# Output projection of head pairs as seven block products instead of eight, in a latent-attention transformer layer

## What is computed

```python
x = x + attn(layernorm(x))          # x: (8, 512, 512)
x = x + ffn(layernorm(x))           # 1536 wide
# attn, for each batch and each of 16 heads:
scores = (q_nope @ k_nope.T + q_pe @ k_pe.T) / sqrt(192)
attn   = softmax(scores, axis=-1)
out    = concat_over_heads(attn @ v)          # 512 tokens x (16 * 128)
return out @ wo.T                             # 512 x 512
```

## Time and profile before

| what | value |
|---|---|
| median of 3 runs | 2230.14 us (2228.98 to 2230.31) |
| span of the profiled execution | 2228.8 us, 1.3 us under the median |
| granted TensorE clock, mean | 0.999 |
| PE busy, matmuls | 2205.4 us, 99%, 10977 |
| DVE, ACT, POOL busy | 70%, 48%, 45% |
| DMA, mean | 98 GB/s |

### The profile page before, as it was taken

One profiled execution on the slowest core, in us unless ns is written; L12 is line 12 of the kernel. 1 busy time (PEld: TensorE's weight loads), 2 busy tenths in 40 slices (PEclk: granted clock), 3 DMA queues, 4 the chain that ended last, 5 costly groups with the idle time before them and its releaser, 6 DMA issues.

```text
span 2228.8 us, 34908 instructions
## 1 busy us (share of the span) xinstructions
PE 2205.4 (99%) x10977; PEld 1026.8 (46%) x10977; DVE 1557.8 (70%) x3227; ACT 1066.6 (48%) x2345; POOL 1001.5 (45%) x688
## 2 busy tenths in 40 slices
PE   7999999999999999999999999999999999999999
PEld 5444544445444454444544445444454445444454
DVE  7888887776477764777648775587755877467773
ACT  6667564554255542555325553355443554345532
POOL 4657465453355524454244642536334363343322
PEclk9999999999999999999999999999999999999999
DMA  7868336562175631756216561365614564145530
GB/s 248 188 124 150 88 71 142 106 124 51 23 151 105 122 53 34 145 105 127 44 43 146 106 121 29 73 123 106 118 25 104 106 115 95 24 104 109 106 65 19
DMA packets 703800, 219.42 MB, mean 98 GB/s; under 512 B 685520, under 2 KB 685776, under 8 KB 702672
## 3 DMA queue, kind: packets, MB, share of 16 engines
q1 hardware_dynamic: 703696, 218.09, 47.7%
HBM read 40.78 MB, written 8.39 MB: 22 GB/s over the span
## 4 chain that ended last, share of the span: by engine, by line
PE 93%; DVE 3%; ACT 1%; DMA 1%; POOL 1%; issue 1%; SPq 0%; DVEq 0%; POOLq 0%
PE bank L853 13%; PE bank L291 11%; PE bank L293 11%; PE bank L292 11%; PE scores L863 7%; PE scores L663 5%; PE scores L293 5%; PE scores L291 5%; PE scores L292 5%; PE bank L674 4%; PE bank L675 4%; PE bank L676 4%; PE scores L660 3%; PE bank L840 1%; PE bank L689 1%; PE scores L557 1%
## 5 line engine op out<-in xcount | busy, mean ns | idle before, releaser
L1716 POOL TENSOR_TENSOR arena<-arena 128x1024 f16<-128x1024 f32 x256 | 545.7, 2132 | 620.3 <-ACT arena L1079 620.3
L1077 ACT ACTIVATE arena<-scores,shift 128x512 f32<-128x512 f32 x512 | 357.5, 698 | 535.0 <-DVE shift L1429 494.8
L1449 DVE SCALAR_TENSOR_TENSOR arena<-bank,rden,arena 128x512 f32<-128x512 f32 x508 | 347.9, 743 | 137.0 <-PE bank L293 137.0
L1427 DVE TENSOR_REDUCE mx<-scores 128x1 f32<-128x512 f32 x512 | 352.5, 689 | 20.5 <-PE scores L293 16.7
L1079 ACT ACTIVATE arena<-scores,shift 128x512 f16<-128x512 f32 x512 | 358.6, 700 | 0.0
L853 PE MATMUL bank<-arena,WFF 128*128 128x512 f16 x1392 | 313.5, 379 | 0.8 <-DVE arena L1601 0.6
L1774 POOL TENSOR_TENSOR arena<-arena 128x512 f16<-128x512 f32 x96 | 114.4, 1191 | 255.6 <-ACT arena L1152 255.6
L853 PEld LDWEIGHTS bank<-arena,WFF 128*128 128x128 f16 x1392 | 135.9, 98 | 164.1 <-DVE arena L1601 2.3
L291 PE MATMUL bank<-WVO,arena 128*128 (+1 forms) x512 | 194.2, 379 | 2.4 <-DVE arena L1222 1.2
L1222 DVE SCALAR_TENSOR_TENSOR arena<-bank,arena 128x512 f16<-128x512 f32 (+1 forms) x263 | 176.2, 670 | 29.1 <-ACT arena L1070 24.4
L663 PE MATMUL scores<-arena 128*128 128x512 f16 x512 | 195.4, 382 | 0.0
(11 more groups left out here) (159 smaller groups left out, 3480.5 us busy)
## 6 DMA issues: line engine op xcount, KB each, us to landing
arena<-arena SPq DMA_TRANSPOSE x712, 3.2
arena<-w_ffn SPq DMA_DIRECT2D x24, 384.0 KB, 3.5
arena<-x SPq DMA_DIRECT2D x8, 1024.0 KB, 5.6
out<-arena SPq DMA_DIRECT2D x32, 256.0 KB, 2.0
arena<-x SPq DMA_DIRECT2D x14, 512.0 KB, 4.4
WVO<-w_o SPq DMA_DIRECT2D x4, 1024.0 KB, 8.2
arena<-w_nope SPq DMA_DIRECT2D x4, 768.0 KB, 9.1
arena<-down_scale SPq DMA_DIRECT2D x8, 256.0 KB, 3.3
```

What stands on the lines that cost most here:

```text
L1077: act.activation(P32[:, t, :], SC[:, t, :], ACT.Exp, scale=EXP_SCALE, bias=shift[:, t:t + 1], accum_out=esum[:, par, t:t + 1]).then_inc(s[ ...
L1427: dve.tensor_reduce(mx[:, t:t + 1], SC[:, t, :], AX_X, ALU.max).then_inc(s["mxr"], 1)
L1449: dve.scalar_tensor_tensor(out=XR[:, t, :], in0=banks[t][:, :], scalar=by[:, t:t + 1], in1=XR[:, t, :], op0=ALU.mult, op1=ALU.add).then_in ...
L1716: pool.tensor_tensor(PL[:, par, two, :], P32[:, two, :], PH[:, par, two, :], ALU.subtract).then_inc(s["pl"], 1)
```

## The change

Heads are taken in pairs (even head e, odd head o), for the first 14 heads of batches 2 to 7; the last two heads of each of these batches, and all of batches 0 and 1, keep the old projection. With the tokens in two halves and the output columns in two halves of 256, a pair's contribution is a 2 x 2 by 2 x 2 block product. It is now formed by seven block products instead of eight, each with 2 x 3 matmuls of 256 columns, from sums and differences of the context blocks (X32, XP) and of the weight blocks.

- **Weights.** In batch 1 POOL forms the four sums of weight blocks of each pair (`block_sums`, ten operations of 256 elements; `block_sums_lo`, one of 1024), ACT their high halves (`sum_hi`), and SP writes seven blocks per pair to DRAM (`w_duo`). From batch 2 on WVO's memory is reused, and SP loads each pair's blocks (the four early ones 512 KB together, the three late ones 384 KB) ahead of use.
- **Softmax sums.** Because heads are now mixed in the products, the reciprocals are applied to the context, where tokens are columns. DVE makes them (`row_of_sums`, three small operations), ACT spreads them (`row_twice`, 1024 elements), SP turns them by a transposing DMA, POOL adds the two halves (`row_sum`), DVE multiplies the context by the row (`context_by_row`).
- **Sums of contexts.** POOL forms them once a pair (`context_sums`, four operations of 256 and a cast of 1024; `context_sums_lo`, one of 1024); ACT and DVE make high and low halves of the plain blocks (`context_hi`, `context_lo`).
- **Order.** In each head PE's values product now comes last, and the products of a pair come one head later than its second context: four early ones in even heads, three late ones in odd heads. DVE adds eight quadrants per pair (`add_block`), four in each head.
- The next input's scaling moves from POOL to DVE and ACT. The head loops of PE and ACT are unrolled from batch 2 on.

```diff
+            def duo_product(j, x, w, k, start):
+                for t in range(2):
+                    dst = DBANK[k][:, t * HB:(t + 1) * HB]
+                    for m, (p, q) in enumerate(((0, 0), (0, 1), (1, 0))):
+                        r = pe.matmul(dst, lhsT=XP[j % 2][:, p, x, tile(t)], rhs=WB[:, q, w, :],
+                                      start=(start and t == 0 and m == 0), stop=(m == 2), skip_group_check=True)
+                return r
+EARLY = [(X_E1, W_B11, 0, True), (X_S1, W_T1, 1, True), (X_O1, W_B21, 2, True), (X_S2, W_T2, 0, False)]
+LATE = [(X_S3, W_T3, 0, False), (X_S4, W_B22, 1, False), (X_O2, W_T4, 2, True)]
+        DBANK = (BO, BT, BC)
+            def duo_early(b, j):
+                n, base = (b - B_PLAIN) * N_DUO + j + 1, b * (NH * NT) + 8 * j
+                pe.wait_ge(s["w_early"], 16 * n)
+                pe.wait_ge(s["ctl"], b * N_CT + 2 * j + 2)
+                pe.wait_ge(s["outr"], base)
+                for k, (x, w, bk, start) in enumerate(EARLY):
+                    if x == X_S1:
+                        pe.wait_ge(s["x_lo"], n)
+                    if x == X_O1:
+                        pe.wait_ge(s["cth"], b * N_CT + min(2 * j + 3, 2 * N_DUO))
+                    if x == X_S2:
+                        pe.wait_ge(s["outr"], base + 1)
+                    duo_product(j, x, w, bk, start).then_inc(s["outp"], 1)
+            # PE
+            def duo_step(b, i):
+                scores(b, i // 2, i % 2)
+                if i >= 4 and i % 2 == 0:
+                    duo_early(b, (i - 4) // 2)
+                elif i >= 5:
+                    duo_late(b, (i - 5) // 2)
+                absorb(i + 2, b * NH + i + 2)
+                values(b, *before(i // 2, i % 2))
+            # in values()
+                if b >= B_PLAIN and dst is BC:
+                    h = pair * 2 + par
+                    pe.wait_ge(s["cth"], n)
+                    pe.wait_ge(s["outr"], b * (NH * NT) + (0 if h < 3 else 8 * ((h - 3) // 2) + (3 if h % 2 else 8)))
+            # DVE
+            def context_by_row(b, i):
+                n, j, par = b * N_CT + i, i // 2, i % 2
+                dve.wait_ge(s["ctp"], n + 1)
+                dve.wait_ge(s["row"], (b - B_PLAIN) * (2 * N_DUO) + i + 1)
+                k = (b - B_PLAIN) * N_DUO + j
+                if par == 0 and k > 0:
+                    dve.wait_ge(s["x_lo"], k)
+                x = X32[:, X_O1:X_O2 + 1] if par else X32[:, X_E1:X_S3 + 1:X_S3 - X_E1]
+                dve.scalar_tensor_tensor(out=x, in0=BC[:, :].rearrange("p (m n) -> p m n", m=2), scalar=1.0 / ROW_SCALE,
+                                         in1=ROW[:, par].rearrange("p (m n) -> p m n", m=2), op0=ALU.mult,
+                                         op1=ALU.mult).then_inc(s["cth"], 1)
+            def duo_step(b, i, part=None):
+                g = b * NH + i
+                if i >= 2:
+                    context_by_row(b, i - 2)
+                    context_lo(b, i - 2)
+                maxima(g)
+                if part in (0, 1, 2):
+                    next_norm(b, part)
+                if i >= 4 and i % 2 == 0:
+                    adds_early(b, (i - 4) // 2)
+                elif i >= 5:
+                    adds_late(b, (i - 5) // 2)
+                row_of_sums(b, i)
+                qa_lo(g + 2, i % 2)
+                if part in (2, 3):
+                    next_norm(b, part + 1)
+            # ACT
+            def duo_step(b, i):
+                context_hi(b, i - 2)
+                probs(b * NH + i, i % 2, False)
+                qa_hi(b * NH + i + 2, i % 2)
+                row_twice(b, i)
+            # POOL, for each head i
+                        if i >= 3 and i % 2:
+                            context_sums(b, (i - 3) // 2)
+                        head(base + i, i % 2, (0,))
+                        if 1 <= i <= 2 * N_DUO:
+                            row_sum(b, i - 1)
+                        head(base + i, i % 2, (1,))
+                        if i >= 3 and i % 2:
+                            context_sums_lo(b, (i - 3) // 2)
+            # POOL, batch 1
+                    if plain and not first and i >= 2:
+                        if i % 2 == 0:
+                            block_sums(i // 2 - 1)
+                        else:
+                            block_sums_lo(i // 2 - 1)
+            # SP, after the transposes of head i
+                    if not plain:
+                        if i < 2 * N_DUO:
+                            row_of_head(b, i)
+                        if i == 0:
+                            early_blocks(b, 0)
+                            late_blocks(b, 0)
+                        elif i >= 4 and i % 2 == 0:
+                            early_blocks(b, i // 2 - 1)
+                        elif i >= 5:
+                            late_blocks(b, i // 2 - 1)
             # PE, last heads of batches 2 to 6
+                if b >= B_PLAIN:
+                    duo_early(b, N_DUO - 2)
                 latent("q", 0)
+                if b >= B_PLAIN:
+                    values(b, final - 1, 1)
                 scores(b, final, 1)
+                    duo_late(b, N_DUO - 2)
                 values(b, final, 0, BQ)
+                if b >= B_PLAIN:
+                    duo_early(b, N_DUO - 1)
+                    duo_late(b, N_DUO - 1)
```

More of the change, by code:

```diff
@@ L259, in build @@
             "gu", "th", "gt", "ft", "fh", "fl", "dn", "yt", "yo", "yv",
+            "t_plain", "t_sum", "t_hi", "t_lo", "t_out", "rdc", "dup", "row_t", "row", "x_hi", "x_sum", "x_lo", "w_early", "w_late",
         )}
@@ L464, in batch @@
                         weight_chunk(chunk_of(i) + 2)
+                if plain and not first:
+                    sums_of_blocks(N_DUO - 1)
                 sp.wait_ge(s["ctp"], (b + 1) * N_CT)
@@ L1098, in attention @@
                 rot_hi(b, N_ROT_FFN)
+                if not plain:
+                    row_twice(b, 0)
                 if first:
@@ L1107, in attention @@
                 qa_hi(base + 3, 1)
+                if not plain:
+                    row_twice(b, 1)
                 if first:
@@ L1709, in keys_rotated_lo, with head @@
                                    ALU.subtract).then_inc(s["kpl"], 1)
-            def head(g, par):
-                for half in range(2):
+            def head(g, par, halves=range(2)):
+                for half in halves:
                     two = slice(2 * half, 2 * half + 2)
@@ new lines, in context_sums, with step @@
+            def context_sums(b, j):
+                k, n = (b - B_PLAIN) * (5 * N_DUO) + 5 * j, b * N_CT + 2 * j
+                def step(to, x, y, op, after):
+                    if after:
+                        pool.wait_ge(s["x_sum"], k + after)
+                    pool.tensor_tensor(to, x, y, op).then_inc(s["x_sum"], 1)
+                pool.wait_ge(s["cth"], n + 2)
+                pool.wait_ge(s["outp"], b * (NH * NT) + 8 * j - 8)
+                x = [X32[:, m] for m in range(N_BLK)]
+                step(x[X_S1], x[X_S3], x[X_O2], ALU.add, 0)
+                step(x[X_S3], x[X_E1], x[X_S3], ALU.subtract, 1)
+                step(x[X_S2], x[X_S1], x[X_E1], ALU.subtract, 0)
+                step(x[X_S4], x[X_O1], x[X_S2], ALU.subtract, 3)
+                pool.wait_ge(s["x_sum"], k + 4)
+                pool.sem_inc(s["turn"])
+                pool.tensor_copy(XP[j % 2][:, 0, X_S3:], X32[:, X_S3:]).then_inc(s["x_sum"], 1)
@@ L1746, in attention, with context_sums_lo @@
+            def context_sums_lo(b, j):
+                pool.wait_ge(s["x_sum"], (b - B_PLAIN) * (5 * N_DUO) + 5 * j + 5)
+                pool.tensor_tensor(XP[j % 2][:, 1, X_S3:], X32[:, X_S3:], XP[j % 2][:, 0, X_S3:],
+                                   ALU.subtract).then_inc(s["x_lo"], 1)
+            def attention(b, last, first, plain):
                 base = b * NH
```

305 lines of the change are left out of this document (267 added, 38 removed).

## The result

The changed kernel takes **2445.0 us** (median of four runs, 2441.1 to 2445.7) against 2230.2 of the kernel before beside it: ratio 1.0955, 95% interval 1.0940 to 1.0971. The profiled execution spans 2443.6 us, 214.8 more than before.

What follows compares the result with a forecast made beforehand. It took PE, busy 99%, as the bound. Gain and waits came to 130.5 us over batches 2 to 6, 23.8 in batch 7, 14 in batch 1: +168 on 2228.8 gave 2398 us, range 2262 to 2470.

Steps and rivals of the forecast that it cites:

- The gain: PE in batches 2 to 7: 42 matmuls of 256 columns replace 24 of 512, saving 0.59 us per pair, 24.6 in all.
- The even heads' wait for x_lo: Even heads: context_by_row waits for GpSimd's low halves, delaying maxima and first add; PE waits about 2.0 us.
- Head 4: Same wait in head 4, with norm statistics between maxima and adds and short heads 1 to 3 before: 5.2 us.
- Head 6: Even-head wait in head 6 of batches 2 to 6: 1.4 us.
- The next rows' scaling on VectorE: Next rows' norm moved from POOL, at most 0.67 us on DVE at head ends, where it waits for PE: costs nothing.
- The odd heads' 0.55: Odd heads: the values product waits for all eight adds, done at 8.4 us against PE's 7.9; PE waits 0.55 us.
- head 5's 1.1: Odd-head wait in head 5, made longer by the norm's aggregates: 1.1 us.
- Start: Start of batches 2 to 7: queued loads delay probability rows; 5.5 us at values(1) and 2.4 at values(2).
- Tail: Head 15: early products of pair 6 wait 3.2 us for x_lo, late ones 1.0 us for adds or the w_late load.
- Batch 1: POOL overloaded by block sums beside next_norm in heads 8 and 10, delaying ACT: 14 us, between 5 and 20.
- More than this: Rival, chance 0.05: DMA late in every head or a lower granted clock in gaps; both together might cost 80 more, 2480.
- Contended low halves: Rival, chance 0.15: odd heads' context_lo waits for a POOL operation, 0.4 us more before the maxima, +12, 2410.

Runs made afterwards that it cites:

- e1: Changed kernel with GpSimd's low halves of the context sums (context_sums_lo) moved from the odd head's end to right behind context_sums: 2419.2 us.
- e7: Changed kernel with the even head's second half written to a block of its own, so VectorE no longer waits for GpSimd's low halves: 2361.4 us.
- e11: e1 with VectorE's third norm part moved from head 5 to 6, and its row tiles from heads 6 to 9 to heads 6 and 8: 2399.4 us.
- e15: e7 with head 15's late blocks before its transposes, first blocks behind head 2's, low halves early in head 15, third norm part after head 6: 2305.3 us.
- e3: Changed kernel with the first pair's weight blocks loaded after head 2's transposes instead of after head 0's: 2422.1 us.
- e12: e13 with e3's later first blocks, the residual load moved from behind head 0's transposes to head 3's, and norm statistics behind the adds: 2383.5 us.
- e13: e7 with e1's early low halves, and head 15's late weight blocks issued before its transposes: 2361.7 us.
- e8: Changed kernel with extra matmuls that nobody reads put into PE's idle places, 82 in each of six batches: 2413.9 us.
- e18: e15 with GpSimd's 1024-wide subtraction for the probabilities' low halves split into four of 256: 2336.4 us.

## Why the prediction was right, and where it was not

The forecast was 2398 us, slower, by waits that take the place of the matmuls saved; it was 47 us (1.9%) short of 2445.

- **The gain** of 0.59 us per pair holds for the bare matmuls (18 in 2.13 us less the last one's run, so 0.109 each). A pair without its wait, in batch 7 of e1, is 10.59 + 11.75 - 0.32 = 22.02 us against 22.44: 0.42 shows. The rest is probably the restart after each wait; no run separates it.
- **The even heads' wait for x_lo** was right in cause and size. Forecast 2.0 to 2.1, measured 2.40, 2.37, 2.19, 2.18 in heads 8 to 14 of batch 3; e7 shows the cause. Head 4: 5.2 forecast, 4.95 measured. Head 6: 1.4 forecast, 2.72 measured; the term lacked VectorE's norm operations behind head 5 (e11, e15), the first of which lasts 1.57 us beside GpSimd. The next rows' scaling on VectorE was priced at 0.67 us at the most and put at nothing; beside GpSimd it takes up to 1.83, and stands behind heads 7 and 9.
- **The odd heads' 0.55** was wrong except for head 7 (0.55), and so was head 5's 1.1 (0.18 measured). The step took maxima every 0.86 us and adds at 0.68, from rows where VectorE was paced by PE. Alone it runs maxima every 0.78 and adds every 0.6, and ends 7.8 us into the head instead of 8.4, before PE's 7.9.
- **Start**: 5.5 + 2.4 = 7.9 forecast. Values of head 1 (asked for in head 2) wait 5.2 to 7.9, those of head 2 (in head 3) at most 0.6. Right in sum, wrongly split. The reason, loads ahead in the queue, is shown by e3.
- **Tail**: 3.2 + 1.0 forecast, 3.26 + 1.29 measured in batch 3, the second a wait for the late blocks.
- **Batch 1**: 14 forecast, 8.6 measured, 6.9 of them in heads 10 (16.57 us) and 12 (12.74), where PE's listed waits are for transposes. The cause was right: GpSimd, busy with block sums and the norm, starts the low halves of head 9 at 456.77, 3.0 us after ScalarE's last exponential, and PE waits for their transposes until 465.06. The backlog was sized too large: head 8 lasts 11.22 us as before.
- **The step that was missing is the clock.** The waits of batch 3 add up to 30.6 us, less 4.1 for the gain 26.5, against 26.1 forecast: that is luck in part, since the errors above cancel. The batch grew by 36.4. The 10 us between are matmuls at a granted 0.50 after the gaps, and restarts; over the kernel the clock cost at least 43.9 us, and the forecast missed 47. The forecast named it in its rival "More than this" and dismissed it with the clock at 1.00 in the first 10 us. That row was the wrong witness: it shows a clock before PE's first matmul, not one after a pause in steady work.
- **Contended low halves**, the rival from the port's rule, had the right mechanism and the wrong operation. The odd heads' low half takes 0.74 us beside GpSimd instead of 0.68, not 0.4 more; in the head shown above it is GpSimd's second sum that takes longer (1.05 us, its neighbours 0.73). The three four-element operations of row_of_sums, priced at 0.6 us together, take 1.6 in the mean (0.17, 0.40 and 1.06). As far as the traces show, that costs PE something only where norm work stands beside them, before heads 6, 8 and 10.

Of the 75 us that e15 still loses, 68 are the waits in the three groups above and 9 those in two smaller ones that the kernel before hardly has, less 24.6 for the gain. That leaves some 22, of which batch 1 has a few (it is 8.3 us longer, in part by waits already counted; no experiment touched it), and the clock 3.3. What the rest is stays open; restarts after some 80 waits would be enough at 0.2 us each, which is an estimate from the 0.17 us missing per pair above.

## What to carry to other kernels

A product on the busiest engine that needs an eighth fewer operations is worth little when the replacement hands the result through four engines inside one head: find what the helpers overwrite for each other, and ask who waits for the buffer and not only for the data. Price a wait on TensorE with what the clock does after it: here a gap of 2.2 to 2.4 us could cost 1.7 more, one of 5 about 3. And fix such waits one at a time with a profile between: twice here a transfer came onto the path with a sound fix. In e1 it was the late blocks, which took back 38 of 62 us of waits; in e12 the residual, moved back together with the weight blocks, and e12 was 22 us slower than e13.

## What the runs showed of the hardware that was not expected

- In a kernel whose PE is over 90% busy, the granted clock fell to 0.50 in or shortly behind 26 of the 47 gaps of over 2 us behind the start, the shortest of 2.07 us, and came back within 7 us. It stayed at 1.00 across others of the same length and longer (2.37, 2.71, 3.26), so the gap's length alone did not decide it. After the 4.95 us gap above it cost about 3 us: 11 matmuls of 512 columns at 0.43 instead of 0.2155, and six of 256 at about twice their 0.109. Filling the gaps with unread matmuls took 31 us off the kernel (e8). The Trainium skill (TensorE: Matmul & The Clock Gate, "Part 1: The HAM clock gate") says that the gate follows how busy the engine has been; by that rule, the trace agrees.
- A VectorE operation on four elements took up to 2.04 us, always until the GpSimd instruction it met had ended (104 of 104 in the kernel after). A 512-element TENSOR_SCALAR from SBUF to SBUF (L1547) takes 0.54 us alone and up to 1.83 beside GpSimd, where it ends 0.28 us behind the instruction that it met; while RECIPROCAL on the same four elements stayed at 0.18.
- Shorter GpSimd instructions shortened the longest wait and not the sum (116.1 us in e15, 117.4 in e18), and four of 256 elements cost 2.73 us for one of 2.13.
